# A drain raises the chunk semaphore in layer 1 of a two-layer graph network kernel

## The reference

```python
edge_index = jnp.stack([src, dst])
x = _layernorm(x + _L0_gnn_ref(x, edge_index, W_l, b_l, W_r))
x = _layernorm(x + _L1_gnn_ref(x, edge_index, W_self, b_self, W_neigh, b_neigh, gamma, beta))
```

## Time and profile before

| | us |
|---|---|
| median of 3 runs | 4253.43 |
| lowest and highest of them | 4247.24, 4258.62 |
| the profiled execution's own time | 4222.63 |
| its span in the profile | 4220.8 |
| TensorE matmul busy in it | 2795.4 (66%) |
| DVE busy in it | 2605.4 (62%) |
| POOL busy in it | 1896.1 (45%) |

### The profile page before, as it was taken

How to read it: one execution, slowest core, us unless ns; L and a number is a source line. 1 busy time by engine, 2 the same in 40 slices (tenths; PEclk the granted TensorE clock), 3 DMA queues, 4 the chain that set the end, 5 groups by cost and what they waited for, 6 DMA issues and landing times.

```text
span 4220.8 us, 57125 instructions
## 1 busy us (share of the span) xinstructions
PE 2795.4 (66%) x11308; PEld 1186.1 (28%) x11308; DVE 2605.4 (62%) x6523; ACT 813.8 (19%) x2156; POOL 1896.1 (45%) x2073
## 2 busy tenths in 40 slices
PE   1000088888888888866999655555555555568887
PEld 1000033333333433322554211111111111124443
DVE  3878877777777777754555444444444444448887
ACT  0300044444444444410222000000000000002222
POOL 0600066666666666664000366666666666630000
PEclk9555599999999999976999766666566665669999
DMA  3300066666666666664333566666666666661111
GB/s 141 123 0 0 21 169 165 170 165 167 167 169 166 168 167 167 168 202 137 102 103 98 160 178 173 179 179 179 177 178 174 180 177 177 172 115 60 55 60 50
DMA packets 201222, 586.38 MB, mean 139 GB/s; under 512 B 34672, under 2 KB 35502, under 8 KB 201196
## 3 DMA queue, kind: packets, MB, share of 16 engines
q0 software_dynamic: 148480, 488.56, 42.6%
q1 hardware_dynamic: 52716, 97.53, 7.1%
HBM read 534.51 MB, written 51.44 MB: 139 GB/s over the span
## 4 chain that ended last, share of the span: by engine, by line
PE 38%; DVE 19%; issue 19%; DMA 8%; DVEq 6%; POOL 2%; another core or an unknown queue 2%; ACT 2%; SPq 2%; POOLq 0%; ACTq 0%
PE ps L710 37%; DMA rows<-table,idx_ring 7%; DVEq L576 4%; DVE acc L583 3%; DVE onehot L569 2%; POOL rows L364 2%; DVE flat L501 2%; DVE flat L502 1%; DVE flat L503 1%; DVE where L598 1%; PE ps L812 1%; DVE st L658 1%; DVE spot L596 1%; PE ps L815 1%
## 5 line engine op out<-in xcount | busy, mean ns | idle before, releaser
L364 POOL DMA_INDIRECT rows<-table,idx_ring x1856 | 1793.8, 966 | 1394.7 <-issue 462.6
L710 PE MATMUL ps<-rows,onehot 128*128 128x512 f16 (+1 forms) x5568 | 1393.7, 381 | 758.0 <-DVE onehot L569 346.3
L583 DVE TENSOR_TENSOR acc<-acc,ps 128x513 f32 x928 | 638.2, 688 | 830.5 <-issue 353.7
L710 PE MATMUL ps<-where,put 128*128 128x464 f16 x3328 | 805.5, 365 | 348.8 <-ACT put L859 291.4
L710 PEld LDWEIGHTS ps<-rows,onehot 128*128 128x128 bf16 x5568 | 526.5, 111 | 1650.1 <-issue 888.2
L569 DVE TENSOR_SCALAR onehot<-iota_node,loc_ring,rows 128x128 bf16<-128x128 f16 x1856 | 586.4, 323 | 297.6 <-DMA rows<-table,idx_ring 253.1
L858 ACT ACTIVATE put<-spot,flat 128x128 f16<-128x128 f16 x832 | 334.1, 402 | 1091.7 <-DVE spot L596 860.7
L710 PEld LDWEIGHTS ps<-where,put 128*128 128x128 f16 x3328 | 268.1, 98 | 659.2 <-issue 351.8
L598 DVE TENSOR_SCALAR where<-iota_chunk,hi_ring 128x928 f16<-128x928 f16 x832 | 378.8, 455 | 0.0
L872 ACT ACTIVATE flat<-acc,rdeg 128x512 f32 (+1 forms) x98 | 69.4, 710 | 1551.2 <-DVE rdeg L647 1547.6
L710 PE MATMUL ps<-w_a,flat 128*128 128x512 f32 x784 | 356.0, 597 | 0.1
(11 more groups left out here) (131 smaller groups left out, 1361.9 us busy)
## 6 DMA issues: line engine op xcount, KB each, us to landing
rows<-table,idx_ring POOLq DMA_INDIRECT x1856
table<-rows SPq DMA_DIRECT2D x98, 257.0 KB, 3.2
h_scratch<-rows SPq DMA_DIRECT2D x49, 256.0 KB, 2.0
rows<-h_scratch SPq DMA_DIRECT2D x49, 256.0 KB, 2.7
acc<-in_x SPq DMA_DIRECT2D x4, 3072.0 KB, 23.5
rows<-in_x SPq DMA_DIRECT2D x48, 256.0 KB, 3.2
out<-rows SPq DMA_DIRECT2D x48, 256.0 KB, 2.0
w_a<-in_w_l_t SPq DMA_DIRECT2D x1, 1024.0 KB
```

Source lines behind the costliest of these rows:

```text
L364: nc.gpsimd.indirect_dma_start(out=rows[:, k % GB, :], out_offset=None, in_=tables[layer][:, :], in_offset=bass.IndirectOffsetOnAxis(ap=id ...
L583: V.tensor_tensor(tile_acc, tile_acc, part, ALU.add).then_inc(s_acc, 1)
L710: return nc.tensor.matmul(*args, skip_group_check=True, **kw)
```

## The change

In layer 0 nothing changes. In layer 1 the last product of a chunk no longer carries the increment of `s_mm`; TensorE gets one more instruction after it, a drain, and that carries it. There are 928 of them, one for each chunk of layer 1, 16 in the body of the loop.

```diff
-                    mm(ps[:, bank + 1, 0:1], lhs, row[:, 2 * D + 2:2 * D + 4].bitcast(bf16)[:, 0:1],
-                       start=start, stop=stop).then_inc(s_mm, 1)
+                    last = mm(ps[:, bank + 1, 0:1], lhs, row[:, 2 * D + 2:2 * D + 4].bitcast(bf16)[:, 0:1],
+                              start=start, stop=stop)
+                    if layer == 0:
+                        last.then_inc(s_mm, 1)
+                    else:
+                        nc.tensor.drain().then_inc(s_mm, 1)
```

## The result

The changed kernel took 4287.26 us in the median of four runs (4285.55 to 4291.66) against 4254.04 us (4247.24 to 4258.62) for the kernel before on the same chip: a ratio of 1.0081, with a 95% interval of 1.0064 to 1.0098. It is slower by 34 us. The forecast had the direction and the stage right and the size too large: 72 us, 4325.

The account below looks back on a forecast made before the run. It took layer 1's chunk loop as bound by a mixture of POOL's pace, DVE's stops and TensorE's runs. Longer TensorE chunks on the chain, 98 or 47 us, middle 72, put the 4253.4 median at 4325 us; range 4260 to 4420.

Parts of the forecast that it names:

- Where the stage stood: Layer 1's chunk loop: gathers take 1375.6 us, 216 us beyond POOL's pace, in a mixture with TensorE's products on the chain.
- The moved signal: In layer 1, s_mm goes up after the drain, so POOL and DVE see each chunk 0.15 us later, at most 0.30.
- The gap that a drain opens: On TensorE in layer 1, each boundary exposes 0.16 us; with the drain a run's chunk grows from 0.88 to 1.19 us.
- the estimate of 162 us: Estimate by the skill's page: each of layer 1's 928 drains costs the hidden 175 ns in full.
- The clock: TensorE's granted clock in layer 1 falls from 0.62 to between 0.50 and 0.58; +0.33 us a chunk at 0.50.
- The sum: Layer 1: 296 chunks on the chain add 98 or 47 us by clock; middle 72 us, hidden and added parts cancelling.
- my first rival: TensorE becomes the bound of layer 1's loop: 27.0 us a trip against 23.7, +190 us, 4445 us; chance 0.17.
- TensorE's own stops from 16 more instructions: 16 more instructions in TensorE's layer 1 loop may lengthen its own stops; counted as nothing and left to the range.
- the signs: Layer 1's chunks take 1430 to 1460 us, no gapless run of six products or more, clock near 0.5, other stages unchanged.
- The ring: Second rival: POOL's ring of eight in layer 1 absorbs the drain, no difference, 4253 to 4263 us; chance 0.14.
- the drain does wait: Denies the third rival: TensorE's drain retires early in layer 1, releasing POOL sooner, 4206 to 4229 us; chance 0.07.

Follow-up runs that it names:

- e9: The changed kernel run again unedited, on a chip where the kernel before took 3779 us: 3844.76 us, ratio 1.0172.
- e12: The kernel before plus, after each layer 1 chunk, a TensorE increment of a semaphore nobody reads, on a chip without stops: 3780.83 us, ratio 1.0003.
- e1: The changed kernel with the drain kept but s_mm raised by the last product again: 4253.06 us, ratio 1.0076 to the kernel before (4221 us).
- e16: The changed kernel with one more product of 384 columns a chunk in layer 1, which nobody reads: 4130.85 us, ratio 1.0922 to the kernel before.
- e14: The changed kernel with one drain for each group of two chunks, on a chip without stops: 3781.32 us, ratio 0.9996 to the kernel before.
- e5: The kernel before plus, after each layer 1 chunk, a TensorE increment of a semaphore nobody reads: 3779.75 us, ratio 1.0003.
- e3: The changed kernel with two drains after each layer 1 chunk, the second raising s_mm: 4248.24 us, ratio 1.0057 to the kernel before (4221 us).
- e4: The changed kernel with TensorE's layer 1 loop written out for 8 chunks instead of 16: 4249.78 us, ratio 1.0068 to the kernel before.
- e2: The changed kernel with one drain for each group of two chunks, on the chip with 4221 us before: 4232.29 us, ratio 1.0028.

## Why the prediction was wrong in its size

**Where the stage stood.** Right: a mixture of POOL's pace, DVE's stops and TensorE's runs, and 216 us beyond POOL's pace. The shares by cause are less sure than they look, as the trace holds only 1466 of the 1856 increments of `s_mm`.

**The moved signal.** Counted with 0.15 us of drain. It comes 0.02 us later than with the product (e9 against e12), and e1 shows that where it sits doesn't matter once the array is waited for.

**The gap that a drain opens.** Too small. I put a chunk of a run at 1.04 + 0.15 = 1.19 us; it is 1.04 + 0.22 or 0.31, 1.30 in the mean. Of the Trainium skill's rule ("TensorE: Matmul & The Clock Gate", Step-by-step: what each phase is for), that the array's emptying hides behind the next product, the trace bears out the direction. The page's 175 ns (its section Single matmul latency) is neither what a drain cost on TensorE, where a chunk of a run grew by 1.30 - 0.88 = 0.42 us, nor what it cost the program: the estimate of 162 us stands against 66 us at most measured, since TensorE had slack against POOL's pace. The 0.11 us that I missed stand across POOL's 1.25, and so they decide which engine is the bound.

**The clock.** Right: 0.50 in the stage, from 0.62. In e16 one more product between the drains didn't bring it back, in e14 pairs without a drain between them did (0.66). That the low clock is why a chunk passes 1.25 us is worked out, not run: 0.61 + 0.27 = 0.88 at the higher level would be under it.

**The sum.** This is the step that failed: "296 chunks on the chain x 0.33 = 98 us, or x 0.16 = 47 us. I take the middle". It takes the loss as a share of the chunks on a chain that otherwise stays as it is, and lets what is hidden and what comes onto the chain cancel. They didn't cancel, and the chain didn't stay: all chunks came onto it, and what had been on it left. That was my first rival, at 0.17. It was right in TensorE as the bound, and wrong in its price of 190 us. It had a trip at 27.0 us; 1419.5 / 58 are 24.5. Of the 2.5 us between them 0.6 are the pace, 16 x 1.30 = 20.8 in place of 21.4. The other 1.9 are in the 5.6 us of DVE's stops, which I let go on beside TensorE's pace. In their place stand 3.7 us a trip: 3.3 of TensorE's own stops and loop ends (176 + 18 us in 58 trips), the rest in gaps a little longer than the commonest. So the stage went from 1160 us of gathers at POOL's pace and 216 beyond them to 1206 at TensorE's pace and 213 beyond, and in e1, on the chip with 4221 us, to 1206 and 196: 46 us more of pace, 20 less of stops, +27 in place of the forecast 72. Where there are no stops to exchange, TensorE's pace and the loop's end show in full, 66 us (e9).

**TensorE's own stops from 16 more instructions.** Left at nothing: on a chip without stops right (e5, e12). With stops no run tells it.

**The range, the signs and the other rivals.** 4287 lies in 4260 to 4420, a range wide enough to hold two mechanisms, so that says little for the sum. The stage was to take 1430 to 1460 us; it took 1419.5, and 1402.4 in e1. The ring did not absorb the drain, and the drain does wait: no run of more than one chunk is left, and a drain lasts as long as its chunk.

**What stays open.** What the stops are, why they come on some chips and not on others, and why DVE's vanish when TensorE paces the loop. With a second drain there are 74 us less of TensorE's (e3 against e1), and a shorter body leaves them. One rival is untested: the writing of the trace may itself hold the engines. The stops come together with missing records. The traces of the changed kernel, of the kernel before and of e1 to e4 hold 22 000 to 25 000 semaphore increments, all the others 45 000 to 46 000, with none of `s_mm` missing. No run here tells whether an execution without a profile would have the stops. On a chip with stops it wasn't shown that the loss goes when TensorE has slack, and e2 speaks against it going in full; on the others it was shown. No version here beats the kernel before.

## What to carry to other kernels

A drain on TensorE after each small batch lays open the end of the array and the start of the next batch, a gap of 0.22 to 0.31 us here. On the chips without stops it cost the program nothing as long as batch and gap stayed under the pace of the slowest other engine; where there were stops, half as many drains with a pace under POOL's still cost 6 to 17 us. So compare the two paces first, before counting instructions on a chain. When a change moves an engine to the edge of becoming the bound, add up the stage anew with that engine in front, and ask which of today's stalls it will cover. And look at the same program on a second chip before a loss or gain of a per cent is called a property of the change: 34 us on one were 66 on another.

## What the runs showed of the hardware

- The kernel before took 4221 and 4254 us in two comparisons and 3779 to 3782 us in four later ones, each of these on another chip. The difference lies in the two loops over chunks: with 4221 us the gathers took 1448 us in layer 0 and 1376 in layer 1, on a chip without stops 1208 and 1172 (e12, with an instruction more), and the rest of the program is as long on both within 2 us. In layer 1 it is in stops of 2 to 5 us, of DVE before the change and of TensorE with drains.
- Of the small instructions of DVE's sequencer in layer 1, 300 of 3790 took over 0.4 us before, most of them 0.7, where on a chip without stops none takes more than 0.32 us (e12).
- A drain on TensorE lasts until the products ahead of it are done, 1.04 us in the median behind a chunk of 1.04 us; a second one right behind it lasts 0.013 us (e3).
- A second drain behind a first adds 0.07 us of gap, 132 - 66 = 66 us over 928 of them.
- TensorE stayed at the lower clock, 0.50, with 741 of 900 us busy in batches of 1.36 us with 0.22 to 0.31 us between (e16), and was granted 0.66 with 634 of 900 us busy in pairs and single chunks (e14).
